# An early-fusion network on one core: the same steps in another order on three engines, with two dummy matmuls added

## The reference, cut to what matters

```python
h = tokens(x)                         # shifted images, 16x16 patches, layernorm folded in, projection to 192
h = concatenate([h, txt], axis=1)     # (16, 96, 192)
h = h + segment_attention(layernorm(h))   # reduce to 96, 12 heads, 4 segments of 24 tokens, softmax
h = h + experts(layernorm(h))             # router over 8 experts, top 2, a capacity for each expert
h = h + linear_attention(layernorm(h))    # l1-normalised q and k, q (k^T v)
h = h + soft_slots(layernorm(h))          # two softmaxes of one set of logits, gelu, two projections
```

## Time and profile before

| | us |
|---|---|
| median of 3 runs | 357.21 (355.73 to 357.46) |
| the profiled execution, its own time | 357.25 |
| its span, first to last instruction | 355.1 |
| first stage ends (first expert matmul) | 128.76 |
| experts end | 252.5 |
| last VectorE instruction | 351.84 |
| TensorE busy | 329.5 (93%) |
| VectorE busy | 205.0 (58%) |
| mean granted clock of TensorE | 0.986 |

### The profile page before, as it was taken

The page is one execution under the profiler, slowest core; times in us unless marked ns, Lnnn a source line. Parts: engine busy times, 40 slices in busy tenths (PEclk is TensorE's granted clock), DMA queues, the critical chain, the costliest instruction groups (busy, mean ns, idle before and its releaser), DMA issues. The chain is left out here.

```text
span 355.1 us, 7978 instructions
## 1 busy us (share of the span) xinstructions
PE 329.5 (93%) x3288; PEld 236.2 (67%) x3288; DVE 205.0 (58%) x639; ACT 99.4 (28%) x208; POOL 49.1 (14%) x119
## 2 busy tenths in 40 slices
PE   4899998987969989999999999999999989899895
PEld 3676566865747437595867759586876766776665
DVE  6925596859797964125324332432354456969864
ACT  1224558464732431011010101101012213332250
POOL 8603354130301020000000000000020011101100
PEclk9999998798999999999999999999999999999999
DMA  7983002404060007999189240000000000000005
GB/s 261 343 215 114 4 3 69 137 3 113 25 169 3 2 8 140 188 196 220 40 200 195 71 133 0 3 0 1 2 2 0 2 0 2 3 0 2 0 2 133
DMA packets 27802, 26.64 MB, mean 75 GB/s; under 512 B 4117, under 2 KB 22935, under 8 KB 27767
## 3 DMA queue, kind: packets, MB, share of 16 engines
q1 hardware_dynamic: 26871, 25.55, 29.2%
q10 hardware_dynamic: 896, 0.59, 0.7%
HBM read 24.86 MB, written 1.28 MB: 74 GB/s over the span
## 5 line engine op out<-in xcount | busy, mean ns | idle before, releaser
L736 PEld LDWEIGHTS banks<-sb_wo_sl,sb_attn_hidT_attn 128*128 128x128 f32 x384 | 62.2, 190 | 5.6 <-issue 4.9
L736 PE MATMUL banks<-sb_wo_sl,sb_attn_hidT_attn 128*128 128x192 f32 x384 | 64.5, 329 | 0.0
L1711 DVE COPY sb_w_tok_e_out<-banks 60x384 f32<-60x384 f32 x32 | 17.8, 555 | 49.8 <-PE banks L736 49.3
L1239 ACT ACTIVATE sb_attn_hidT_attn<-banks 128x480 f32<-128x480 f32 x24 | 13.6, 570 | 102.9 <-PE banks L723 102.9
L718 PE MATMUL banks<-sb_tok_xeT,sb_wi_sl 128*128 128x480 f32 x96 | 40.1, 568 | 1.1 <-ACT sb_tok_xeT L1224 1.1
L1701 DVE TENSOR_SCALAR sb_attn_hidT_attn<-banks 128x480 f32<-128x480 f32 x24 | 15.8, 658 | 27.8 <-PE banks L723 25.9
L718 PEld LDWEIGHTS banks<-sb_tok_xeT,sb_wi_sl 128*128 128x128 f32 x96 | 18.0, 190 | 18.9 <-issue 17.0
L503 PE MATMUL banks<-sb_tok_xeT 128*32 128x193 f32 (+1 forms) x512 | 25.2, 328 | 0.0
L723 PE MATMUL banks<-sb_tok_xeT,sb_wi_sl 64*128 64x480 f32 x96 | 21.5, 580 | 0.0
L503 PEld LDWEIGHTS banks<-sb_tok_xeT 128*32 128x32 f32 (+1 forms) x512 | 17.2, 109 | 6.0 <-issue 3.4
L756 PE MATMUL banks<-sb_w_tok_e_out,sb_onehot_combT 128*64 128x192 f32 x192 | 16.9, 330 | 0.1
(11 more groups left out here) (238 smaller groups left out, 535.4 us busy)
## 6 DMA issues: line engine op xcount, KB each, us to landing
sb_wo_sl<-in_wo SPq DMA_DIRECT2D x16, 288.0 KB, 3.7
sb_tok_xeT<-in_xin SPq DMA_DIRECT2D x8, 448.0 KB, 6.2
sb_onehot_combT<-route_rows SPq DMA_DIRECT2D x6, 512.0 KB, 9.3
sb_wi_sl<-in_wi SPq DMA_DIRECT2D x8, 288.0 KB, 3.2
sb_wi_sl<-in_wi SPq DMA_DIRECT2D x24, 96.0 KB, 3.3
sb_xn<-route_rows SPq DMA_DIRECT2D x4, 512.0 KB, 11.6
sb_w_tok_e_out<-in_wtok SPq DMA_DIRECT2D x2, 960.0 KB, 6.8
sb_attn_hidT_attn<-route_rows SPq DMA_DIRECT2D x2, 512.0 KB, 12.9
```

What stands on the lines that cost most here:

```text
L736: mm = nc.tensor.matmul(PS[:, 4 + j // 2, j % 2 * D:(j % 2 + 1) * D], hidT[:, e % 2, f, j * 128:(j + 1) * 128], wo_sl[:, q, f], start=(f = ...
L1239: nc.scalar.activation(hidT[:, e % 2, f].rearrange("f (g c) -> f g c", g=PAIRS)[:, :, 0:CAP], PS[:, HID_BANKS[f], 0:SLOTS].rearrange("f (g ...
L1711: ve.tensor_copy(e_out[64 * (e % 2):64 * (e % 2) + CAP, hf * 4 + z:hf * 4 + z + 3:2, e // 2], PS[64 * z:64 * z + CAP, 4 + hf, 0:2 * D].rea ...
```

## The change

No step is altered and, but for two calls of `keep_busy`, none is added or removed. The calls at the end of the TensorE, ScalarE and VectorE blocks are written in another order, in the first and the second stage. The waits `free(...)` move with the steps or keep their place. GpSimd's and SyncE's queues stay as they are, and so does the loop over the experts. The diff, cut to the places that matter here (TensorE, then ScalarE, then VectorE):

```diff
             weight_sums()
-            patches(1, 0)
             free(sums=1)
             square_rows(0)
+            square_sums(0)
             spread_sums()
-            square_sums(0)
+            square_rows(1)
+            patches(1, 0)
             patches(1, 1)
-            square_rows(1)
-            free(tok_mid=2, tok_var=2)
-            patches(2, 0)
             square_sums(1)
...
-            dispatch(0)
             free(a_oT=3)
             project(2)
+            dispatch(0)
             free(r_counted=2)
             free(xeT=2)
+            keep_busy(0, 512)
             free(a_h=3, r_part=3)
             turn_weights(3, 0)
             turn_weights(3, 1)
+            keep_busy(0, 256)
+            free(a_probT=11)
+            weigh_values(3, 0)
             free(a_probT=10)
             turn_weights(3, 2)
-            free(a_probT=11)
-            weigh_values(3, 0)
...
             soft_inputs(3)
-            soft_hidden(3, 4)
             slot_outputs(0)
             slot_outputs(1)
+            soft_hidden(3, 4)
+            slot_outputs(2)
             token_outputs(0)
-            slot_outputs(2)
             token_outputs(1)
+            token_outputs(2)
             slot_outputs(3)
-            token_outputs(2)
             token_outputs(3)
...
             keep_soft_inputs(3)
+            gelu_slots(0, 0, 3)
             exp_slots(3)
             exp_tokens(3)
-            gelu_slots(0, 0, 3)
             keep_slots(3)
             gelu_slots(1, 3, 4)
...
             choose(0)
-            scale_routes(0)
-            route_norm(0)
+            score_norm(1, 2)
             score_max(2, 0)
             score_max(2, 1)
+            route_norm(0)
+            score_max(2, 2)
             place(0)
```

More of the change, by code:

```diff
@@ L931, in _ @@
             turn_inputs(0)
-            patches(2, 1)
+            free(tok_mid=2, tok_var=2)
+            patches(2, 0)
             free(a_xnT=1)
             reduce_inputs(0)
+            patches(2, 1)
+            free(a_xl=1)
+            keys(0)
+            values(0)
             square_rows(2)
             queries(0)
-            free(a_xl=1)
-            keys(0)
+            square_sums(2)
             free(x_ss=3)
             square_rows(3)
-            square_sums(2)
-            values(0)
             free(tok_mid=4, tok_var=4)
@@ L947, in _ @@
             patches(3, 0)
+            free(a_sub=3)
+            turn_projection()
             free(a_xnT=2)
@@ L950, in _ @@
             patches(3, 1)
-            square_sums(3)
-            queries(1)
             free(a_xl=2)
             keys(1)
-            free(a_sub=3)
-            turn_projection()
+            square_sums(3)
             turn_weights(0, 0)
+            route_projection()
+            queries(1)
             free(tok_mid=8, tok_var=8)
             values(1)
-            route_projection()
+            free(a_kexp=8, a_qT=2)
+            turn_inputs(2)
             free(a_vexp=9)
@@ L966, in _ @@
             turn_weights(0, 2)
-            turn_inputs(2)
+            free(a_xnT=3)
+            reduce_inputs(2)
             free(a_probT=2)
@@ L971, in _ @@
             weigh_values(0, 2)
-            free(a_xnT=3)
-            reduce_inputs(2)
+            free(a_xl=3)
+            keys(2)
             free(a_oT=1)
@@ L976, in _ @@
             queries(2)
-            free(a_xl=3)
-            keys(2)
             free(a_vexp=18)
@@ L985, in _ @@
             scores(2)
+            free(a_probT=5)
+            weigh_values(1, 0)
+            turn_inputs(3)
             free(a_vexp=27)
@@ L1871, in _ @@
             token_rows(2)
+            token_write(2)
             token_rows(3)
-            token_write(2)
             token_write(3)
@@ L1881, in _ @@
             score_max(0, 1)
+            score_max(0, 2)
             token_write(5)
@@ L1885, in _ @@
             score_norm(0, 1)
-            score_max(0, 2)
             first_norm(2)
-            score_norm(0, 2)
             token_rows(6)
             token_rows(7)
+            keep_projection()
+            score_norm(0, 2)
             token_write(6)
@@ L1943, in _ @@
             choose_first(3)
+            scale_routes(2)
             choose(3)
             route_norm(3)
+            scale_routes(3)
+            place(3)
             mark_slots(2)
-            place(3)
             mark_slots(3)
             keep_tails(0)
-            scale_routes(3)
             keep_tails(1)
@@ L2001, in _ @@
             soft_moments(1)
+            token_shift(0)
+            scale_queries(2)
+            soft_norm(1)
             token_weights(0)
-            soft_norm(1)
             key_norms(3)
+            soft_max(1)
             add_linear(2, 0)
-            soft_max(1)
+            slot_weights(1)
             add_linear(2, 1)
-            slot_weights(1)
             token_shift(1)
@@ L2013, in _ @@
             scale_queries(3)
+            own_heads(3)
             soft_norm(2)
-            own_heads(3)
             token_weights(1)
+            add_linear(3, 0)
             soft_max(2)
+            add_linear(3, 1)
+            slot_weights(2)
+            soft_moments(3)
+            soft_norm(3)
             token_shift(2)
-            slot_weights(2)
-            add_linear(3, 0)
-            add_linear(3, 1)
-            soft_moments(3)
             token_weights(2)
-            soft_norm(3)
             soft_max(3)
+            slot_weights(3)
             token_shift(3)
-            slot_weights(3)
-            token_weights(3)
             keep_own(0, 0, 3)
             add_up_bias(0)
+            token_weights(3)
             keep_own(1, 3, 4)
             add_up_bias(1)
+            add_up_bias(2)
             add_soft(0)
-            add_up_bias(2)
             add_soft(1)
+            add_soft(2)
             add_up_bias(3)
-            add_soft(2)
             add_soft(3)
```

178 lines of the change are left out of this document (85 added, 93 removed).

## The result

The changed kernel takes 354.31 us, the median of 8 executions (353.93 to 355.81), the kernel before on the same chip 357.25 (8, 355.73 to 359.04). The ratio is 0.9922, with a 95% interval of 0.9896 to 0.9947: faster by 0.5 to 1.0%. The forecast was 354.0 in a range of 351.5 to 358.9.

What follows compares the result with a forecast made beforehand. TensorE was busy 93% of the span, losing time to half-clock stretches and waits chased with VectorE. 357.25 - 6.1 (first stage) - 1.15 (second) + 3.0 (tail) = 353.0, plus 1.0 held back: 354.0 us, range 351.5 to 358.9.

Steps and rivals of the forecast that it cites:

- The decisive place: VectorE, first stage: scale_routes(0)'s 3.40 us wait for GpSimd's root gets filled; with the other waits, experts 6.1 us earlier.
- The clock in the first stage: TensorE, first stage: full clock from 55 to 116 us, where two stretches had run at about half.
- The rivals in which it falls once more, or as before: First stage clock: falling once more gives 355.7 to 357.3 us, chance 0.20; as before gives 358.9 us, chance 0.12.
- The head: Start of the first stage: uncovered TensorE waits cost 0.6 us (bounds 0 and 1.5); VectorE begins near 26.2.
- The dummies: TensorE, last group's weight turns, first stage: two dummies priced at 0 on the path; without cover they cost 1.3 us.
- The second stage: Up to the last logits: 1.15 us earlier (bounds 0 and 2), with a 1.9 us TensorE wait for soft_inputs(2).
- The rival that it lets the clock fall: Second stage: clock falls behind the 1.9 us wait before soft_inputs(2), costing 2.7 us, total 361.6; chance 0.08.
- The tail: After the last logits: early gelu makes three table loads, exp 2.5 us late; last VectorE instruction 3.0 us later (1.0 to 5).
- The table loads: ScalarE, tail: each change between gelu and exp costs one load of 1.28 us and nothing beside it.
- the rival that rested on it: ScalarE, tail: every table switch has a second part of 1.28 us, two on the path add 2.6: 356.6 us; chance 0.06.
- the hand-overs: Between engines: 1.0 us held back for about ten new hand-overs at 0.1 each.

Runs made afterwards that it cites:

- two dummies that raise the clock: Kernel before the change plus two 256-column dummy matmuls in TensorE's waits ahead of values(1) and route_projection(): 356.01 us, ratio 0.9962.
- the kernel with the old tail: Changed kernel with the old order on all three engines from the last softmax of the slots on: 350.95 us, ratio 0.9779.
- the narrow dummies: New first stage, old second stage, the two dummies at the last group's weight turns cut from 512 and 256 columns to 8 each: 350.26 us.
- the covered wait: New first and second stage, old tail, the 256-column dummy behind soft_inputs(2) replaced by one of 512 ahead of it: 350.57 us.
- the kernel with the early gelu: New first stage and old second stage, with only ScalarE's gelu_slots(0, 0, 3) moved ahead of the last two exps: 354.72 us.

## Why the prediction was right, point by point

- **The decisive place.** Right. The wait for the root went, the first stage gave 6.0 for the 6.1 predicted, and the kernel with this half alone measured 351.25, which is 357.25 less 6.0. But I had put the gain down to VectorE's chain alone and taken the clock as a condition. The runs say that the gain is made of both: two dummies that raise the clock give 1.4 us without any new order, and the one run of that kernel at nearly full clock leaves 3.6 us to the order. That 6.0 comes so near to 6.1 is in part luck: the mark before the change was at 128.76 in one execution and at 127.28 in another with the same first stage. By the medians the first stage gave 6.3 (357.57-351.25).
- **The clock in the first stage.** The forecast had it at full from 55 to 116, and so it was in the profile. In the four kernels with the new first stage, TensorE's instructions at the turns in place and no long wait behind, all 21 runs had a mean clock of 0.998 or more. The rivals in which it falls once more, or as before, did not come in. TensorE's waits from 44 to 129 us, 10.1 us before, came to 5.8, less than the 7.5 that I had found.
- **The head.** Mis-sized. I charged 0.6 us; the scores of group 0 start at 44.94 against 44.93 before. VectorE begins at 25.68, not 26.2, and TensorE at `scores(0)` had been waiting 0.37 us for ScalarE, which now is not there.
- **The dummies.** Wrong in size. They were priced at 0 because VectorE was to be the later one. It is so at `add_attention(3)`, where VectorE arrives 0.4 us after `project(3)` (106.27 against 105.86). But two steps ahead of it, at `place(2)`, VectorE had waited 1.33 us for counts that stand behind the dummies on TensorE; without the dummies this wait is 0.4 us. They cost 0.6 to 0.7 us at the first expert matmul and 0.9 to 1.0 by the medians. VectorE's waits came to 2.7 us instead of 1.9 for this reason; the head's 0.6 paid for it.
- **The second stage.** 0.64 us instead of 1.15. Its wait of 1.9 us before `soft_inputs(2)` came out at 1.73. The rival that it lets the clock fall is real, in about half of the runs of the kernel with the old tail, but costs 1.5 us and not the 2.7 that I gave it, since in the profiled one the low clock lasts over the L874 of `soft_inputs(2)` (2.73 us instead of 1.55), the dummy of 256 columns (1.06 instead of 0.60) and hardly any of `soft_hidden(0, 3)` (2.86 instead of 2.82).
- **The tail.** Three loads, the exp 3.6 us behind the logits, TensorE waiting 2.21 us: as written. The sum, 3.98 instead of 3.0, hides two errors. The last L874 and the first L899 took 2.87 and 1.76 us where they took 1.47 each before: 1.7 us are the clock's, which I had weighed for the wait of 1.9 us at `soft_inputs(2)` and not for the longer one here. The order itself costs the other 2.3 us, less than the 3.0 that I had walked. One run of the changed kernel without its two dummies had this tail and no fall: 351.81 us at a mean clock of 1.000, against 350.16 to 350.32 with the old tail and the dummies. With 0.6 to 1.0 us for the dummies the order comes to 2.1 to 2.7 us, an estimate from that one run. And I had read the loads as nearly the whole cause; with two of them gone the gelu is late all the same, because VectorE's new order holds up `exp_tokens(3)`, and the loss was gone when all three engines had their old tail back; nothing between the two was run.
- **The table loads.** The second load ends at 335.50 and the exp starts at 335.52; the first ends at 333.15 and the gelu starts at 333.16. Nothing is behind them. The Trainium skill (ScalarE: Activation LUTs, "What ACT_TABLE_LOAD costs") gives a drain of about 1.38 us beside each load. None of the switches in these traces shows one, neither behind the load nor ahead of it (the copy ends at 331.85, the first load starts at 331.87; the gelu ends at 334.20, the second starts at 334.22), and the rival that rested on it is out.
- **The number as a whole.** Inside the range and 0.3 us from the forecast (354.31 and 354.0), with errors in five terms that nearly cancel: the dummies and the tail cost more and the second stage gave less than written, the head and the hand-overs cost less. The mechanism of each stage was right; that the sum is so near is luck.

## What to carry to other kernels

Split a reordering by stage and run the halves: this one was a gain of 6 us and a loss of 3 under one median. An order is a set of fits between engines: here one engine's line was put back alone, and the wait turned up one step later. And price each wait of TensorE like those here (1.4 to 2.2 us) twice, once as idle time and once as a possible fall of the clock behind it; a dummy put into such a wait was free, while the two at the turns, where another engine waits for what stands behind them, cost 0.6 to 1.0 of their 1.7 us.

The best kernels here are those with the new first stage and the old tail: 350.26 us with the narrow dummies, 350.57 with the covered wait, 3.5 to 4 below the changed kernel. The two edits together were not run.

## What the runs showed of the hardware that was not expected

The clock's fall behind a wait of 1.73 us is a matter of chance: with the same instructions it came in three of six runs (by their mean clock). Behind the 2.2 us in the tail it came in seven of twelve runs of the kernel with the early gelu. In the changed kernel the mean clock was 0.989 to 0.995 in all eight runs, so it fell in each, though only the profiled one shows where. In the profile of the kernel with the early gelu the clock then stayed at 0.50 for 9 us in which TensorE was busy for 8.54. Before the change it fell at 59.6 us behind gaps of at most 0.48 us between short matmuls, in one execution and not in another of the same instructions; two dummies in these gaps made falls rarer. The new first stage with the old tail has a spread of 0.7 us (350.96 to 351.65), the kernels whose clock falls in some runs and not in others 1.8 to 8.5 us: here the spread itself was a sign of the clock. The length of the waits does not tell it alone: without the two dummies the same kernel has no wait of TensorE over 1.2 us between 44 and 129 us, and its clock fell in two of six runs.
